# An image network's first step folded into its first layer, and its last layer written by channels

## The reference

```
x = coords @ fc0_w + fc0_b                      # coords: 32 x 64 x 64 x 3; 32 channels
x = transpose(x, (0, 3, 1, 2))
for sw, cw, cb in four layers:
    x_ft = rfft2(x, norm='ortho')               # only 20 x 20 frequencies are kept
    x1 = irfft2(einsum('bixy,ioxy->boxy', x_ft[:, :, :20, :20], sw) put into zeros)
    x2 = einsum('bchw,oc->bohw', x, cw) + cb
    x = gelu(x1 + x2)
x = transpose(x, (0, 2, 3, 1))
x = gelu(x @ fc1_w + fc1_b)                     # 32 -> 64
return (x @ fc2_w + fc2_b)[..., 0]              # 64 -> 1
```

## Time and profile before

| what | value |
|---|---|
| median of three runs | 4450.04 us (4443.79 to 4450.76) |
| the profiled execution | 4450.9 us, span 4448.7 us |
| TensorE, VectorE, ScalarE, POOL busy | 84%, 56%, 12%, 17% of the span |
| first image transposes, first half and second half | 30.00 us, 935.78 us |
| first mixing product, first half and second half | 115.65 us, 1020.80 us |
| final products of the first half | 796.14 to 935.78 us |
| next stage's first load (end of the image network) | 1846.58 us |

### The profile page before, as it was taken

One profiled execution on the slowest core, in us unless ns is written; L12 is line 12 of the kernel. 1 busy time (PEld: TensorE's weight loads), 2 busy tenths in 40 slices (PEclk: granted clock), 3 DMA queues, 4 the chain that ended last, 5 costly groups with the idle time before them and its releaser, 6 DMA issues. The chain is left out here.

```text
span 4448.7 us, 109537 instructions
## 1 busy us (share of the span) xinstructions
PE 3744.6 (84%) x44268; PEld 3132.7 (70%) x44268; DVE 2504.3 (56%) x8138; ACT 549.9 (12%) x1173; POOL 740.6 (17%) x1900
## 2 busy tenths in 40 slices
PE   6999999999999999697656566687998878859587
PEld 5898988769989887454424455687997778857444
DVE  4454545145455452223756888888787887852413
ACT  0101011310010112211211110101001000001011
POOL 1000000000000000000002434334343332332021
PEclk9999999999999999777855555555555555556589
DMA  1010000000000000100003110111000000021111
GB/s 37 16 17 2 16 2 16 2 6 16 2 16 16 2 1 2 25 0 4 0 10 91 32 35 29 31 29 31 26 25 32 22 29 24 22 75 46 21 39 27
DMA packets 189736, 96.97 MB, mean 22 GB/s; under 512 B 139463, under 2 KB 172535, under 8 KB 188632
## 3 DMA queue, kind: packets, MB, share of 16 engines
q1 hardware_dynamic: 183574, 84.19, 8.1%
q10 hardware_dynamic: 4626, 7.39, 0.4%
q0 software_dynamic: 1280, 2.10, 0.2%
HBM read 76.11 MB, written 15.96 MB: 21 GB/s over the span
## 5 line engine op out<-in xcount | busy, mean ns | idle before, releaser
L349 PEld LDWEIGHTS im_acc<-im_cwt,im_chan 128*128 128x128 f32 x2048 | 268.7, 191 | 123.0 <-issue 117.3
L468 ACT ACTIVATE im_a<-im_acc 128x512 f32<-128x512 f32 x256 | 152.9, 597 | 1376.7 <-PE im_acc L349 1376.7
L204 POOL DMA_DIRECT2D image_rows<-im_ho x16 | 9.6, 603 | 1761.2 <-DVEq L459 1761.2
L445 DVE COPY im_chan<-im_ring 128x512 f32<-128x512 f32 x192 | 132.8, 692 | 286.8 <-PE im_ring L296 286.8
L346 PE MATMUL im_acc<-im_u,im_e 97*128 97x512 f32 x512 | 265.3, 599 | 7.6 <-DVE im_u L439 7.6
L349 PE MATMUL im_acc<-im_cwt,im_chan 128*128 x2048 | 270.1, 274 | 0.0
L258 PE MATMUL im_ring<-im_d,im_a 128*128 128x128 f32 (+1 forms) x2048 | 242.5, 281 | 19.1 <-issue 12.9
L258 PEld LDWEIGHTS im_ring<-im_d,im_a 128*128 128x128 f32 x2048 | 239.5, 198 | 22.1 <-issue 18.5
L1641 PE MATMUL sc_ps<-H,sc_cols 128*128 128x128 f32 x768 | 231.2, 457 | 11.9 <-POOL H L1528 11.5
L439 DVE COPY im_u<-im_ring 80x512 f32<-80x512 f32 x256 | 171.6, 685 | 118.8 <-PE im_ring L290 118.8
L406 DVE COPY im_half_t<-im_ring 128x480 f32<-128x480 f32 x192 | 168.5, 903 | 116.5 <-PE im_ring L258 116.5
(11 more groups left out here) (394 smaller groups left out, 7460.3 us busy)
## 6 DMA issues: line engine op xcount, KB each, us to landing
sc_g_row<-mem_g_rows_dram SPq DMA_DIRECT2D x96, 256.0 KB, 3.5
im_wbd<-in_c_mix_dram SPq DMA_DIRECT2D x32, 400.0 KB, 6.1
sc_w_row<-mem_w_rows_dram SPq DMA_DIRECT2D x192, 64.0 KB, 2.5
sw_g_all<-sw_gates SPq DMA_DIRECT2D x8, 768.0 KB
mem_hist_h_dram<-sc_hist_h ACTq DMA_DIRECT2D x6, 512.0 KB, 3.0
mem_hist_dz_dram<-sc_hist_dz ACTq DMA_DIRECT2D x6, 512.0 KB, 3.7
mo_hist_dz<-mem_hist_dz_dram SPq DMA_DIRECT2D x8, 384.0 KB, 6.4
mo_hist_h<-mem_hist_h_dram SPq DMA_DIRECT2D x8, 384.0 KB, 6.5
```

The costliest lines, as they stand in the source:

```text
L349: mm = MM(acc[:, p % 2, m:512:4], chan[:, p % 2, m * 128:(m + 1) * 128], cwt[:, bass.ds(l, 1), :].rearrange("p a c -> p (a c)"), start=Fal ...
L468: nc.scalar.activation(a[:, g, :, :].rearrange("p c (w x) -> p (c w) x", x=32)[:, :, p * 4:p * 4 + 4], acc[:, p % 2, :].rearrange("p (c m) ...
```

## The change

The input step goes. The first layer now transforms the three coordinates and a constant row instead of 32 channels: `rows_first` makes three products a group straight from the loaded pixels, and a row of ones, transformed once, stands as the fourth coordinate in `rows3`; `columns_first` makes the same 20 products a group as before, with 16 columns of weights where there were 128; `to_channels` multiplies the kept frequencies of the four coordinates (`freq`, 16 partitions) by the first step's weights (`spread`), seven products. In the accumulation of the first layer, the channel step takes the pixels (`xt`, turned by `turn_pixels`, one fill a group) with the product of both weights (`fc0`, now made on the chip from the tables `lin` and `place`). So every image is loaded twice in a half, and the first layer has no `turn_activations`. The four layers are written out one after the other on TensorE; VectorE and ScalarE keep a loop over layers 1 to 3 and 0 to 2.

In the last layer `u` becomes the stationary operand and `e2` the moving one, and the channel step is one product of 512 columns with the weights stationary, so that `a` is filled with partitions of channels by four columns. The final products then take `a` as their moving operand as it lies, without transposes and copies.

```diff
+                def columns_first(f, g):
+                    for b2 in range(2):
                         ps = fill(f)
+                        for k in range(KG):
+                            for r in range(2):
+                                o = (b2 * 2 + r) * 20 + k * 4
+                                mm = MM(ps[0:16, k * 80:k * 80 + 128], rows3[:, g % 2, o:o + 4, :].rearrange("p n c -> p (n c)"), d2[:, r, :], start=r == 0, stop=r == 1)
                         mm.then_inc(filled, 1)
+                def to_channels(f):
+                    for m in range(0, KG * MO, 16):
+                        ps, n = fill(f), min(16, KG * MO - m)
+                        MM(ps[:, 0:n * 32], spread[:, :], freq[:, m:m + n, :].rearrange("p m b -> p (m b)"), start=True, stop=True).then_inc(filled, 1)
...
-                    with pe.Fori(0, NL) as l:
-                        f = Fills(at, l * LAYER_FILLS)
+                    for l in range(NL):
+                        f = Fills(at + (FIRST_FILLS + (l - 1) * LAYER_FILLS if l else 0))
...
+                                if l == 0:
+                                    MM(acc[:, p % 2, :], e2[0:97, :], u[:, p, :, :].rearrange("p o w -> p (o w)"), start=True, stop=True, skip_group_check=True)
+                                    pe.wait_ge(prepared, ONES_READY[half])
+                                    have(f.base + pixels_at[g])
+                                    for w in range(4):
+                                        mm = MM(acc[:, p % 2, :].rearrange("p (o w m) -> p w o m", w=4, m=4)[:, w], xt[:, g % 2, w, :], fc0[:, p, :, :].rearrange("p o m -> p (o m)"), start=False, stop=True, skip_group_check=True)
+                                elif l == NL - 1:
+                                    for m in range(4):
+                                        MM(acc[:, p % 2, m * 128:(m + 1) * 128], u[:, p, :, :].rearrange("p o w -> p (o w)")[:, m:512:4], e2[0:97, :], start=m == 0, stop=True, skip_group_check=True)
+                                    have(f.base + turned[p])
+                                    mm = MM(acc[:, p % 2, :], cwt[:, l, :], chan[:, p % 2, :], start=False, stop=True, skip_group_check=True)
...
-                            turn_activations(f, g, 4 * q)
                             pend = []
                             for p in range(4):
-                                if p < 3:
-                                    turn_activations(f, g, 4 * q + p + 1)
-                                have(start + p + 1)
+                                pixels = a[:, g, :, :].rearrange("p c (w x) -> p (c w) x", x=32)[:, :, (4 * q + p) * 4:(4 * q + p + 1) * 4].rearrange("p j m -> p m j")
                                 for v in range(2):
...
-                                    MM(acc[:, v, :], fc1[:, v, :], chan[:, p % 2, :], start=True, stop=True).then_inc(acc_full, 1)
+                                    MM(acc[:, v, :], fc1[:, v, :], pixels, start=True, stop=True).then_inc(acc_full, 1)
```

More of the change, by code:

```diff
@@ L80, in image_weights @@
     one = np.eye(4, dtype=np.float32)
[L81 to L84, removed]
+    lin = np.concatenate([fc0_w, fc0_b[None]]).astype(np.float32)
+    rows = np.zeros((97, C), np.float32)
+    rows[0:96], rows[96] = np.tile(fc0_w, (32, 1)), fc0_b
+    place = np.concatenate([np.repeat(np.eye(32, dtype=np.float32), 3, axis=0), np.ones((1, 32), np.float32)])
+    spread = np.zeros((KJ, 4, KJ, C), np.float32)
+    for j in range(KJ):
+        spread[j, :, j] = lin
     mix = np.stack([a.reshape(C, C, KJ, KG * MO).transpose(2, 0, 3, 1) for a in sw])
@@ L238, in have, with image, first_weights @@
                     pe.wait_ge(drained, n + RING)
-                def input_layer(f, half):
-                    for g in range(NGRP):
-                        n = half * NGRP + g
-                        pe.wait_ge(xi_in[n % 2], 32 * (n // 2 + 1))
+                def image(n):
+                    pe.wait_ge(xi_in[n % 2], 32 * (n // 2 + 1))
+                    return xi[:, n % 2, :, :].rearrange("p c x -> p (c x)")
+                def first_weights():
+                    pe.wait_ge(prepared, 4)
+                    MM(acc[0:97, 0, 0:C], lin[:, 0:97], lin[:, 97:97 + C], start=True, stop=True).then_inc(prepared, 1)
+                    MM(acc[:, 1, 0:128], one, d1[:, :], start=True, stop=True).then_inc(prepared, 1)
@@ L253, in rows_transform, with turn_pixels @@
+                def turn_pixels(f, g, half):
+                    ps, src = fill(f), image(half * 2 * NGRP + NGRP + g)
+                    for q in range(4):
+                        mm = T(ps[0:96, q * 128:(q + 1) * 128], src[:, q * 96:(q + 1) * 96], ident[:, :])
+                    mm.then_inc(filled, 1)
+                    return f.n
                 def rows_transform(f, g):
@@ L435, in _ @@
                                 turned(g, k)
+                        if first:
+                            V.memset(xt[96:97, :, :, :], 1.0).then_inc(prepared, 1)
+                            pixels(0)
                         for g in range(NGRP):
@@ L439, in _ @@
                                 V.tensor_copy(u[0:80, :, q:q + 4, :], src).then_inc(drained, 1)
-                            if g:
+                            if g and not first:
                                 for p in range(2):
@@ L443, in _ @@
                             for p in range(PH):
-                                if p + 2 < PH:
+                                if first and p == 2 and g + 1 < NGRP:
+                                    pixels(g + 1)
+                                if not first and p + 2 < PH:
                                     V.tensor_copy(chan[:, p % 2, :], drain(f)).then_inc(drained, 1)
```

160 lines of the change are left out of this document (98 added, 62 removed).

## The result

| | before | after |
|---|---|---|
| median of 4 runs each, us | 4448.35 (4443.79 to 4450.76) | 4516.67 (4511.02 to 4525.22) |
| ratio, 95% interval | 1 | 1.0150 (1.0136 to 1.0164) |
| profiled execution: us, span | 4450.9, 4448.7 | 4525.22, 4523.5 |
| its granted clock, mean | 0.754 | 0.711 |

The change makes the kernel 1.5% slower, where 4266 us and "faster" had been forecast. Start with the page. Its part 1 answers to the earlier trace rows (busy us, share of the span, instructions); the other line is from its part 2, the granted clock in 40 slices of 113 us, in tenths.

The account below looks back on a forecast made before the run. TensorE was taken to set the end wherever the diff touches; -9 -54.6 -54.6 -15.6 -17 -39.7 +6 = -184.5 from 4450.9 us gave 4266 us, with its own range 4246 to 4287 (chance 0.64) and a wider one of 4243 to 4330.

Parts of the forecast that it names:

- Setup, -9: Before the network starts: three small tables loaded instead of 388 KB of first-step weights, -9 us.
- First image product to first mixing product: Start of the image network in each half: fewer products and transposes on TensorE, -54.6 us a half.
- clock in the new first step, +6: Channel products on 16 rows, with waits around them, may lose the clock: 3 us a half, +6 in all.
- Rest of the first layer, -7.8 in each half: First layer's accumulation: 24 transpose fills leave, 3 pixel fills enter, a longer VectorE wait adds 1.5; -7.8 us a half.
- Loop written out, -17: TensorE's idle time at the six loop-backs, before the row transform, goes without a branch: -17 us.
- Last layer by channels, 0: Last layer: one 512-column and four 128-column products change places, weights read at a 16-byte step; no cost, 0 us.
- Final products, -39.7: Final products: 16 groups lose 2.48 us of transposes each; fc1's moving operand at 128 bytes taken as free; -39.7 us.
- B: New first step: clock stays at 1.2 GHz throughout, about +42 us, 4308 us; chance 0.13.
- Rival A: Final products: the moving operand at a step is slow, +56 us (4322) or, at double time, +110 (4376); chance 0.11.
- Rival D: Clock falls in all that becomes thin, final products included: +200 to +260, about 4490 us, slower than before; chance 0.03.

Follow-up runs that it names:

- the contiguous version: Changed kernel, but with the last layer's stationary tiles and the final products' moving operand both laid out contiguously and in order: 4260.86 us, ratio 0.9557 to the kernel before.
- the run with a step for each group: Changed kernel with last-layer tiles and final-product operands read at 4, 8, 16 and 128 bytes in image groups 0 to 3: 4432.97 us, one run.

## Why the prediction was wrong

By the start of the first layer norm behind the image network, 1866.95 us before, the prediction's sum puts the changed kernel at 1682.5. It came at 1930.74, 248 us later; with contiguous operands it came at 1671.00. The steps, in the prediction's order:

- *Setup, -9*: the first row products came at 19.80, as forecast from POOL's memset. Right.
- *First image product to first mixing product*, with the *clock in the new first step, +6*: 52.55 us for a forecast of 52 and 3 for the clock, and 33.65 for 30.4 and 3. Right, -2 in all; the granted clock of 0.95 and 0.86 is the clock's part, and the pixels at a 12-byte step, 24 passes a half at 0.207 us for 0.112, are 2 us that no term had.
- *Rest of the first layer, -7.8 in each half*: only 3.2 of it came, +9 in all. From the first mixing product of the first layer to that of the second it takes 174.2 us in both halves, and 177.4 where the layers are written out in the kernel before. The longer wait for VectorE came as forecast (1.79 us instead of 0.78), but the clock's loss went on behind the first step, where the term for the clock had stopped: the mixing takes 25.4 us instead of 22.4, its first 5.45 at 0.50, and the products behind the wait lose another 1.7, at 0.68 (shown above).
- *Loop written out, -17*: right in kind, too small. The waits are there as read, but each also takes the clock down for the next products: -31.
- *Last layer by channels, 0*: **wrong**, the first failed step. The four tiles at a 16-byte step take 1.86 us instead of 0.89, 0.97 x 64 = +62 us in the changed kernel. With the tiles alone mended, 56 us came back.
- *Final products, -39.7*: **wrong**, the second and the larger failure. "I take 0, since the row is of the same engine and kind of read" is the sentence that failed: the row was of transposes, and the products are of another kind. The forecast was 139.64 - 19.85 = 119.8 us a half; 118.4 is what the contiguous version takes, and 217.5 what the changed kernel takes: +98 a half, +195 in all. Taken in this order, half of it is the step: at full clock 1.77 + 0.83 = 2.60 us a product with its second products, for 1.76. Half is the clock: 3.42 for 2.60, almost all of it in the second products, 0.83 to 1.54, which have no step at all.

-2 +9 -14 +62 +195 = 250, for 248. The run with the first step folded and the end as before shows the smaller terms together: 149 us gained for a forecast of 144.8 (184.5 without the 39.7). This is nearer than the terms by themselves, since the loops' and the first layer's misses have opposite signs: luck in part. Two sums on the way to the forecast are off and change nothing: a load of 15.5 us issued at 4.93 ends at 20.4 and not at 24, and B's 26 + 20 - 6 is 40.

Rival A had the place and, at its upper end, the size of the step's own price (double time of 128 products, +110, as shown). It did not carry on to what the slow stream does to the clock, and it did not look at the last layer, where the same rule held. Rival D had the sign and a total of about 4490, and its +200 to +260 holds the 250 that was missed, but it gave the wrong cause: with no transposes and contiguous operands the clock holds 0.97, or 1.00 where the second products never stand 16 in a row. The two should have been one chain, the step first and the clock behind it, and 0.03 for its sign was too little. The Trainium skill, "SBUF — State Buffer", in the section on the DMA port swizzle, was weighed and set aside for one row. The runs agree with its sentence that full bandwidth needs at least two hits in a 16-byte line: 8 bytes are nearly free (198 ns for 192), 12 bytes cost part of the price (262), 16 and 128 the whole of it (329 and 313). They do not agree with the same section where it calls a step of four fp32 elements free: that is the 16 bytes.

What stays open: why transposes read at a step at full rate; and why, with contiguous operands, most dips at a row of 16 pass (0.89, then 1.00) and a few last to the end of the stage (0.50 from 1600 us on in the run with only the final products contiguous, and from 741 us on in the first half of the run with a step for each group).

## What to carry to other kernels

Before an operand is read where it lies, to save a copy or a transpose, give it a price from a row of the same kind of instruction at that step; weight loads of transposes say nothing on those of products. If no such row exists, the writer of the operand can often lay it out contiguously at no cost, as ScalarE and VectorE could here: the same instructions on TensorE, some 264 us apart by the ratios. And where a stream becomes slower, ask what the clock does to everything that shares the engine with it, since that doubled the loss in the final products here.

## What had not been expected of the hardware

- An fp32 product's stationary tile of 128 columns loads in 192 ns contiguous, 198 at 8 bytes, 262 at 12, 329 at 16 and 313 at 128; a transpose's at 128 bytes in 189.
- A moving operand of 512 fp32 columns takes 0.94 us for its two passes, from its start to the next row's, contiguous at 2.4 GHz, 0.98 at 8 bytes, 1.85 at 16 bytes and 1.77 at 128; at 1.2 GHz 1.85 contiguous and 1.87 to 1.95 at a step.
- The same contiguous final products ran for whole groups at 1.00 (14.4 us) or at 0.50 (27.3 us), by what had run ahead of them, with TensorE busy all the time in both; and putting a product of fc1 between every 8 passes of second products held it at 1.00 for the whole stage.
- A loop's turn-round cost TensorE 3 to 7 us a layer, of which the idle time that the list of waits shows is little more than half.
